# Low-rank rows: transposes spread over later tiles' products, copies in a home of their own, block numbers requested by ScalarE

## The chip, the cores and the metric

The kernel runs on one NeuronCore of a Trainium2 chip. The metric is the device time of one execution in microseconds (us); less is better. Engines are called PE (TensorE), PEld (its weight loads), ACT (ScalarE), DVE (VectorE), POOL (GpSimd) and SP (SyncE, which here only issues DMAs). ACTq and SPq are the DMA-issuing sides of ACT and SP.

## What is computed

`x` has 32 blocks of 32 rows by 512. Four layers are added to it, one after the other; each has a part that is chosen by a number that belongs to the block:

```python
x = x + einsum('bct,bcd->bdt', x, L0_weights[itok_B_0_15])   # L0: one of 16 weights, 32 x 32, per block
base  = einsum('bsi,oi->bso', x, W)                  # L1: one dense 512 x 512 ...
low   = einsum('bsi,bir->bsr', x, lora_A[label])     #     ... and low-rank rows, rank 32, 5 labels
delta = einsum('bsr,or->bso', low, lora_B) * 0.5
x = x + base + delta
x = x + einsum('bsi,boi->bso', x, weight[adapter])   # L2: one of 8 weights, 512 x 512, per block
x = x + attention(x, k_cache, v_cache, block_table, cache_seqlens)   # L3: projections, rotary, attention
```

L3 takes most of the time; the change lies in L0 and L1.

## The kernel before, in words

`stage_layers` does L0, L1 and L2 and prepares L3. The 1024 rows of `x` are TT = 8 tiles of P = 128 rows, four blocks to a tile; KC = 4 chunks of 128 make a row of 512. The stage is one block of code with a stream of its own for each engine; the streams meet at its end (line 271), and the rest of the kernel (`stage_project_attend_output`) begins only then.

The order of the work is a list, `uses` (lines 202 to 210). Each entry is one use of a PSUM bank; entry n has bank `ps[n % 8]`, and PE waits before it until entry n - 8 has been drained (line 359). PE ends each entry with one count on `written`. PE, ACT and DVE all walk the same list in the same order, each doing its own share of an entry. The kinds of entries are:

- ("L0", t): x times the L0 weights of tile t (line 365); DVE adds the bank to x (line 579). The weights of a tile are four 32 x 32 blocks that DVE (tiles 0 to 3, line 549) and ACT (tiles 4 to 7, line 424) copy out of `w0_all` by block number. Both wait first for both DMAs of `idx`, the block numbers (`idx_in`, 32), and read them into registers, then for `w0_all` itself.
- ("x1T", t): four transposes of x (line 369); ACT and DVE split the result into a high and a low part (lines 446 and 587).
- ("low", t): twelve products with `lora_A` of all labels (`a_hi`, `a_lo`); DVE keeps those of the block's own label (line 601) and adds them up into `low` (line 604).
- ("lowT", t): one transpose of `low` (line 382); DVE copies it into `low_t` (line 608).
- ("L1", t): twelve products with W and then one with `bw_t`, the padded `lora_B`, by `low_t` (line 392); DVE adds the bank to x (line 579).
- ("x2T", t): four transposes; ACT copies them into `x2t` (line 472).
- ("L2", t): 64 products, 4 blocks by 4 chunks by 4 (line 402). The weights of blocks 0 to 2 of a tile are copied by DVE and ACT out of `w2t` (`pick`, lines 434 and 537). Those of block 3 come by a DMA of 1 MB that SP issues (`fetch`, line 291), in three buffers; the first is `w1n`.

`low_t` and `bw_t` lie in the room of `a_n`, `a_hi` and `a_lo` (`after_a`), which the low products read. POOL clears `bw_t` (line 330) after the last of them, then fills it (line 333, `bw_ready`).

Before the entry ("L1", 0) DVE runs a block of work that doesn't belong to the list's tiles (lines 557 to 563): `angles`, two `reduce`, and then the first three picks. `angles` also waits for four small DMAs that ACT issues. Its results go to ACT (two sines, line 461), whose results go to POOL (eight tables, line 341, `tables_made`); `w1n` holds the intermediate values. SP waits for `tables_made` 8 before it issues `fetch(0)`, since `fetch(0)` overwrites `w1n`; `fetch(1)` and `fetch(2)` come behind it in SP's order, after the last L1 product.

PE waits before the first product of ("L2", 0) for `x2_turned`, `fetch(0)` and the first picks (lines 394 to 399).

## Time and profile before

| | us |
|---|---|
| median of three runs | 1190.09 |
| lowest and highest | 1187.87, 1191.71 |
| profiled execution, its own time | 1188.03 |
| its span in the profile | 1186.2 |
| busy in the span: PE | 1166.4 |
| DVE | 851.5 |
| POOL | 727.6 |
| ACT | 687.1 |

The profile is of one execution. Its span runs from the first to the last instruction; 1.8 us lie around it. The layers' stage takes the first 105 us of it. Times in the rows are microseconds from the start of the span; "idle before" is how long the engine had done nothing, and the releaser is whatever the profile saw last before it went on. It names one releaser where an instruction waited for several.

### The profile page before, as it was taken

Reading aid. Unit: us, or ns where it says so; the run is one execution under the profiler, and the core shown is the slowest. Engines: PE = TensorE matmul, PEld = TensorE weight load, DVE = VectorE, ACT = ScalarE, POOL = GpSimd, SP = SyncE. Lnnn points to the kernel's source line nnn. Section 1 sums busy time; section 2 is a strip of 40 time slices with the busy share of each in tenths; the row PEclk is TensorE's granted clock in tenths of the full one; section 3 lists DMA queues with packets and bytes.
Section 4 is the critical chain, followed back from the end, with each engine's and each line's share of the span. In section 5 each row is a group of like instructions: output and inputs, shape, how many; then the busy total and the mean of one; then the engine's idle time right before and its main releaser. Section 6 shows DMA issues by size and latency. Waiting matters only on the chain.

```text
span 1186.2 us, 27883 instructions
## 1 busy us (share of the span) xinstructions
PE 1166.4 (98%) x8138; PEld 1030.1 (87%) x8138; DVE 851.5 (72%) x1746; ACT 687.1 (58%) x1647; POOL 727.6 (61%) x566
## 2 busy tenths in 40 slices
PE   7999999999999899999999999999999999999998
PEld 5746888888888799999999999999999998787877
DVE  7878687777866977877878778887788878722222
ACT  4175444344444577777777777777777778412111
POOL 1403999999999765555555555555555556344442
PEclk9999999999999999999999999999999999999999
DMA  9385544534446689999999999999999999876773
GB/s 340 137 279 196 147 134 134 143 82 133 133 125 190 169 256 304 293 298 302 297 301 298 292 304 295 302 296 294 304 295 301 291 334 323 267 218 208 223 212 115
DMA packets 254401, 283.67 MB, mean 239 GB/s; under 512 B 56053, under 2 KB 208629, under 8 KB 254358
## 3 DMA queue, kind: packets, MB, share of 16 engines
q1 hardware_dynamic: 237270, 234.38, 67.6%
q10 hardware_dynamic: 17088, 48.76, 13.5%
q8 instruction: 21, 0.34, 0.1%
q14 instruction: 22, 0.18, 0.1%
HBM read 236.78 MB, written 46.27 MB: 239 GB/s over the span
## 4 chain that ended last, share of the span: by engine, by line
PE 52%; POOL 21%; issue 7%; DMA 5%; DVE 3%; ACT 2%; SPq 0%; ACTq 0%; POOLq 0%; DVEq 0%
PE early_pair L1237 19%; PE early_pair L1212 10%; PE early_pair L109 7%; PE early_pair L110 6%; PE early_pair L111 6%; POOL prj_rstd L1146 6%; POOL prj_qn L1148 5%; POOL prj_ta L1136 5%; DMA all_room_a<-inv_scratch 5%; PE early_pair L1244 3%; POOL prj_rs L1140 3%; POOL all_room_a L1176 2%; DVE out_o_lo L1537 2%; ACT out_o_hi L1728 1%; DVE out_wo_lo L1521 1%
## 5 line engine op out<-in xcount | busy, mean ns | idle before, releaser
L1604 ACT ACTIVATE att_prob<-att_neg,att_nmax 128x544 f32<-128x544 f32 x256 | 192.1, 750 | 115.9 <-DVE att_nmax L1369 91.0
L1369 DVE CUSTOM_DVE_ANT_1 att_neg<-att_mask,early_pair 128x576 f32<-128x576 f32 x256 | 192.1, 751 | 83.3 <-PE early_pair L111 67.5
L1156 POOL TENSOR_TENSOR att_k_lo<-all_room_a,att_k_hi 128x544 fp32r<-128x544 f32 x123 | 165.8, 1349 | 135.4 <-ACT att_k_hi L1630 135.4
L1156 POOL TENSOR_TENSOR att_k_lo<-att_kT,att_k_hi 128x544 fp32r<-128x544 f32 x128 | 173.9, 1359 | 105.5 <-ACT att_k_hi L1630 105.5
L1421 DVE COPY att_pT<-early_pair 128x512 f32<-128x512 f32 x256 | 175.8, 687 | 28.3 <-PE early_pair L1212 28.3
L109 PE MATMUL early_pair<-att_k_hi,att_q_lo 128*128 128x288 f32 (+1 forms) x512 | 168.8, 330 | 1.5 <-DVE att_nmax L1369 1.5
L1212 PE MATMUL early_pair<-all_ident,att_prob 128*128 128x128 f32 x1024 | 157.0, 276 | 0.0
L110 PE MATMUL early_pair<-att_k_lo,att_q_hi 128*128 128x288 f32 (+1 forms) x512 | 147.4, 288 | 0.0
L111 PE MATMUL early_pair<-att_k_hi,att_q_hi 128*128 128x288 f32 (+1 forms) x512 | 147.2, 288 | 0.0
L1176 POOL TENSOR_TENSOR all_room_a<-all_room_a 128x1024 f32<-128x1024 f32 x31 | 78.9, 2545 | 98.7 <-DMA all_room_a<-inv_scratch 98.7
L1237 PE MATMUL early_pair<-att_pT,att_vc 128*128 128x128 f32 x1024 | 135.4, 275 | 0.6 <-ACT att_ost L1761 0.6
L1237 PE MATMUL early_pair<-att_pT,all_room_b 128*128 128x128 f32 x1024 | 135.3, 275 | 0.0
L1212 PEld LDWEIGHTS early_pair<-all_ident,att_prob 128*128 128x128 f32 x1024 | 116.3, 140 | 20.9 <-issue 13.6
L1641 ACT ACTIVATE prj_sq<-early_pair 128x512 f32<-128x512 f32 x64 | 38.3, 599 | 165.5 <-PE early_pair L111 161.4
L1237 PEld LDWEIGHTS early_pair<-att_pT,att_vc 128*128 128x128 f32 x1024 | 124.5, 192 | 0.9 <-ACT att_ost L1761 0.8
L1237 PEld LDWEIGHTS early_pair<-att_pT,all_room_b 128*128 128x128 f32 x1024 | 124.5, 192 | 0.0
L1537 DVE TENSOR_TENSOR out_o_lo<-all_room_a,out_o_hi 128x1024 fp32r<-128x1024 f32 x31 | 41.1, 1325 | 107.7 <-ACT out_o_hi L1728 107.7
L1136 POOL TENSOR_TENSOR prj_ta<-prj_ta,prj_tb 128x640 f32<-128x640 f32 x64 | 101.1, 1579 | 9.1 <-DVE prj_tb L1471 9.0
L109 PE MATMUL early_pair<-out_wo_hi,out_o_lo 128*128 128x512 f32 x256 | 101.1, 395 | 2.5 <-DVE out_o_lo L1537 2.4
L1728 ACT ACTIVATE out_o_hi<-all_room_a 128x1024 fp32r<-128x1024 f32 x31 | 32.8, 1060 | 120.9 <-POOL all_room_a L1176 120.9
L111 PE MATMUL early_pair<-out_wo_hi,out_o_hi 128*128 128x512 f32 x256 | 99.8, 390 | 0.0
L110 PE MATMUL early_pair<-out_wo_lo,out_o_hi 128*128 128x512 f32 x256 | 99.8, 390 | 0.0
(164 smaller groups left out, 2928.7 us busy)
## 6 DMA issues: line engine op xcount, KB each, us to landing
all_room_a<-in_k_cache_t SPq DMA_DIRECT2D x256, 128.0 KB, 5.9
att_kT<-in_k_cache_t SPq DMA_DIRECT2D x256, 128.0 KB, 6.8
all_room_b<-in_L_cond_v_cache SPq DMA_DIRECT2D x136, 128.0 KB, 4.2
q_scratch<-prj_qst SPq DMA_DIRECT2D x64, 256.0 KB
att_vc<-in_L_cond_v_cache SPq DMA_DIRECT2D x128, 128.0 KB, 4.0
att_vc<-in_L_cond_v_cache ACTq DMA_DIRECT2D x128, 128.0 KB, 5.1
all_room_a<-o_scratch SPq DMA_DIRECT2D x31, 512.0 KB, 3.8
all_room_a<-inv_scratch SPq DMA_DIRECT2D x31, 512.0 KB, 5.5
```

What stands on the lines that cost most here:

```text
L109: pe.matmul(out, w_lo, x_hi, start=first, stop=False)
L110: pe.matmul(out, w_hi, x_lo, start=False, stop=False)
L111: return pe.matmul(out, w_hi, x_hi, start=False, stop=last)
L1136: g.tensor_tensor(ta[s][:], ta[s][:], tb[s][:], ALU.add).then_inc(pool_step, 1)
L1146: g.tensor_tensor(rstd[s][:], rs[s][:], power[:], ALU.pow).then_inc(pool_step, 1)
L1156: g.tensor_tensor(k_lo[j % SPLITS][:], kT[j // HK % 2][:, :, j % HK, :], f32(k_hi[j % SPLITS][:]), ALU.subtract).then_inc(k_split, 1)
L1176: g.tensor_tensor(o_n[s], o_n[s], inv_rows[s], ALU.mult).then_inc(o_scaled, 1)
L1212: t = pe.transpose(bank[:, c * P:(c + 1) * P], p[:, c * P:(c + 1) * P], ident[:])
L1237: pe.matmul(o, vc[s][:, c, cols], pT[j % 2][:, c, :], start=(c == 0 and j % PAIR == 0), stop=False)
L1369: v.tensor_tensor_reduce(halves[0], halves[1], scores_of(j, n)[:, :, 0:KA], 1.0, 3.0e38, ALU.add, ALU.min, nmax[j % 2][:]).then_inc(maxed, 1)
L1421: v.tensor_copy(pT[j % 2][:], pt[bank_of(j)][:].rearrange("p (c q) -> p c q", c=NCH)).then_inc(kept, 1)
L1604: act.activation(prob[j // GROUP % 2][:, j % GROUP, :], neg[j % 2][:, 0:KEYS], ACT.Exp, bias=nmax[j % 2][:, 0:1], scale=-1.0, accum_out=to ...
```

## The change

- **Order.** `uses` puts ("lowT", t - 3) behind ("low", t) for t from 3 on, and ("lowT", 5) to ("lowT", 7) behind ("L1", 0). Before, all eight transposes stood between the last low product and the first L1 product. The number of entries is the same.
- **Home.** `low_t` moves out of the room of the `lora_A` parts into the parts of `w2a` that belong to block 3, which the picks don't use.
- **Waits.** PE waits for `low_t` and `bw_t` only ahead of the last product of an L1 entry, no longer ahead of its first.
- **Side work.** DVE's `angles`, `reduce` and first picks, and ACT's sines and first picks, move from ahead of ("L1", 0) to ahead of ("L1", 1).
- **Block numbers.** The two DMAs of `idx` leave SP's queue, where they stood ahead of those of `x`. ACT issues them, one ahead of and one behind that of `w0_all`.

```diff
--- before.py
+++ after.py
@@ -128,7 +128,6 @@
         a_hi = m.sb("a_hi", [P, KC, LR], F32R)
         a_lo = m.sb("a_lo", [P, KC, LR], F32R)
         after_a = Region(nc, "lay", at_a, nc.sbuf_base - at_a)
-        low_t = after_a.sb("low_t", [P, TT, P])
         bw_t = after_a.sb("bw_t", [P, H])
         bw_n = m.sb("bw_n", [R, H])
         lab_i = m.sb("lab_i", [P, B], I32)
@@ -147,6 +146,8 @@
         spare = spare_a[:, 0:2 * H], spare_b[:, 0:2 * H]
         picked = [[w2a[:, r, b] for b in range(BT)] for r in range(2)]
         picked.append([x[:, i * H:(i + 1) * H] for x in spare for i in range(2)])
+        FETCHED = BT - 1
+        low_t = [w2a[:, i // KC, FETCHED, i % KC * P:(i % KC + 1) * P] for i in range(TT)]
         w0_all = w2a[:, 0, 0].rearrange("p (s d) -> p s d", s=NS0)
         x2t = [low[:, i * KC:(i + 1) * KC, :] for i in range(2)]
 
@@ -202,9 +203,10 @@
         uses = [("L0", 0)]
         for t in range(TT):
             uses += ([("L0", t + 1)] if t + 1 < TT else []) + [("x1T", t)]
-        uses += [("low", t) for t in range(TT)]
-        uses += [("lowT", t) for t in range(TT)]
-        uses += [("L1", t) for t in range(TT)] + [("x2T", 0)]
+        for t in range(TT):
+            uses += [("low", t)] + ([("lowT", t - 3)] if t >= 3 else [])
+        uses += [("L1", 0)] + [("lowT", t) for t in range(TT - 3, TT)]
+        uses += [("L1", t) for t in range(1, TT)] + [("x2T", 0)]
         for t in range(TT):
             uses += ([("x2T", t + 1)] if t + 1 < TT else []) + [("L2", t)] + ([("x3T", t - 1)] if t else [])
         uses += [("x3T", TT - 1)]
@@ -221,7 +223,6 @@
                 return split_lo, split_no[u]
             return {"low": low_ready, "lowT": lowt_ready, "x2T": x2_turned}[kind], i + 1
 
-        FETCHED = BT - 1
         BY_ACT, BY_DVE = ((1,), (1, 2), (1,), (1,)), ((0, 2), (0,), (0, 2), (0, 2))
 
         def share_of(share, g):
@@ -272,8 +273,6 @@
 
             @block.sync
             def _(sp):
-                sp.dma_start(idx[:, 0, :], inp["itok_B_0_15"].rearrange("(a b) -> a b", a=1)).then_inc(idx_in, 16)
-                sp.dma_start(idx[:, 1, :], inp["itok_B_3_7"].rearrange("(a b) -> a b", a=1)).then_inc(idx_in, 16)
                 x_rows = inp["x"].rearrange("(t b) c h -> (b c) t h", b=BT)
                 for i in range(X_PARTS):
                     part = slice(i * TT // X_PARTS, (i + 1) * TT // X_PARTS)
@@ -383,13 +382,13 @@
                     elif kind == "L1":
                         pe.wait_ge(split_lo, split_no[("x1T", i)])
                         pe.wait_ge(w1_lo_done, KC)
-                        pe.wait_ge(lowt_ready, i + 1)
-                        pe.wait_ge(bw_ready, 1)
                         tok = slice(i * P, (i + 1) * P)
                         for k in range(KC):
                             three_pass(pe, bank[:], xT_hi[:, k, tok], xT_lo[:, k, tok], w1_hi[:, k, :], w1_lo[:, k, :],
                                        k == 0, False)
-                        end(u, pe.matmul(bank[:], low_t[:, i, :], bw_t[:], start=False, stop=True))
+                        pe.wait_ge(lowt_ready, i + 1)
+                        pe.wait_ge(bw_ready, 1)
+                        end(u, pe.matmul(bank[:], low_t[i], bw_t[:], start=False, stop=True))
                     elif kind == "L2":
                         pe.wait_ge(x2_turned, i + 1)
                         pe.wait_ge(w2_fetched[i % RING], (i // RING + 1) * 16)
@@ -415,7 +414,9 @@
 
             @block.scalar
             def _(act):
+                act.dma_start(idx[:, 0, :], inp["itok_B_0_15"].rearrange("(a b) -> a b", a=1)).then_inc(idx_in, 16)
                 act.dma_start(w0_all, inp["w0_t"]).then_inc(w0_all_in, 16)
+                act.dma_start(idx[:, 1, :], inp["itok_B_3_7"].rearrange("(a b) -> a b", a=1)).then_inc(idx_in, 16)
                 act.wait_ge(idx_in, 32)
                 state = states(mybir.EngineType.Activation, W0_TILES["act"])
                 act.wait_ge(w0_zero, 1)
@@ -455,7 +456,7 @@
                         act.dma_start(len_i[:], inp["itok_B_207_1644"].partition_broadcast(P)).then_inc(rope_in, 16)
                         act.dma_start(nw[:, 0, :], inp["L3_cond_q_norm_w"].partition_broadcast(P)).then_inc(rope_in, 16)
                         act.dma_start(nw[:, 1, :], inp["L3_cond_k_norm_w"].partition_broadcast(P)).then_inc(rope_in, 16)
-                    elif kind == "L1" and j == 0:
+                    elif kind == "L1" and j == 1:
                         act.wait_ge(reduced, 2)
                         for angles in trig:
                             act.activation(angles, angles, ACT.Sin).then_inc(trig_done, 1)
@@ -553,7 +554,7 @@
                     bank, kind, j = ps[i % 8], *u
                     if u == ("x1T", TT - 2):
                         labels()
-                    if u == ("L1", 0):
+                    if u == ("L1", 1):
                         angles()
                         reduce(0, 0.0, 0.0)
                         reduce(1, 0.25, 0.5 * np.pi)
@@ -605,7 +606,7 @@
                                         ALU.add).then_inc(low_ready, 1)
                     elif kind == "lowT":
                         dve.wait_ge(written, i + 1)
-                        v.tensor_copy(low_t[:, j, :], bank[:, 0:P]).then_inc(lowt_ready, 1)
+                        v.tensor_copy(low_t[j], bank[:, 0:P]).then_inc(lowt_ready, 1)
 
 
 def pages_of(nc, table, b, first, count, engine):
```

## Rows read from the trace of the kernel before

**Rows 1.** the page: busy time and share of TensorE, and the chain that ended last by engine

```profile
PE 1166.4 (98%) x8138; PEld 1030.1 (87%) x8138; DVE 851.5 (72%) x1746; ACT 687.1 (58%) x1647; POOL 727.6 (61%) x566
...
PE 52%; POOL 21%; issue 7%; DMA 5%; DVE 3%; ACT 2%; SPq 0%; ACTq 0%; POOLq 0%; DVEq 0%
```

**Rows 2.** waits of SP's queue, 0 to 110 us: waiter, releaser, us in total, times, longest

```profile
SPq L271 <- PEq L271: 3.0, 1, 3.0
```

**Rows 3.** busy time by stretch: PE, PEld, DVE, ACT, POOL, PEclk, DMA share, GB/s

```profile
30.00:40.00 10.00, 8.67 (x43) 6.64 (x42) 8.12 (x34) 0.00 (x0) 2.01 (x2) 1.00 1.01 372
```

**Rows 4.** timeline, 30 to 37 us: start us, us, engine, line, what [idle before <-releaser]

```profile
30.57 0.75 PEld L382 LDWEIGHTS early_pair<-all_ident,lay_low 128*128 128x128 f32 x7
...
33.16 0.19 PEld L109 LDWEIGHTS early_pair<-lay_w,early_xT_lo 128*128 128x128 f32 x1 [1.24 <-DVE lay_low_t L608]
...
35.79 0.41 PEld L392 LDWEIGHTS early_pair<-lay_bw_t,lay_low_t 128*128 128x128 f32 x2
...
36.45 0.19 PEld L109 LDWEIGHTS early_pair<-lay_w,early_xT_lo 128*128 128x128 f32 x1 [0.24 <-issue]
...
36.02 1.02 PE L392 MATMUL early_pair<-lay_bw_t,lay_low_t 128*128 128x512 f32 x2
...
30.85 0.52 POOL L330 MEMSET lay_bw_t<- 128x512 f32 x1 [16.99 <-PE early_pair L111]
31.56 1.49 POOL L333 TENSOR_SCALAR lay_bw_t<-lay_bw_n 32x512 f32<-32x512 f32 x1 [0.19 <-POOL lay_bw_t L330]
...
31.58 1.66 DVE L608 COPY lay_low_t<-early_pair 128x128 f32<-128x128 f32 x8
33.16 0.14 DVE L507 TENSOR_SCALAR lay_row_i<-lay_pos_i 128x1 int32<-128x1 int32 x1
34.44 0.75 DVE L512 CAST lay_pos<-all_len_i 32x8 f32<-32x8 int32 x4 [0.95 <-DMA lay_w1n<-in_L_cond_k_norm_w]
```

**Rows 5.** timeline, 46 to 64 us, from the tables to the first L2 product

```profile
46.16 10.94 POOL L341 TENSOR_TENSOR early_tabs<-lay_w1n 128x512 f32<-128x512 f32 x8 [13.12 <-ACT lay_w1n L461]
...
57.28 0.40 SPq L291 DMA_DIRECT2D lay_w1n<-in_w_t  x1
...
58.84 0.69 DVE L579 TENSOR_TENSOR all_room_a<-all_room_a,early_pair 128x512 f32<-128x512 f32 x1 [1.80 <-PE early_pair L392]
...
62.90 1.09 ACT L472 ACTIVATE lay_low<-early_pair 128x512 f32<-128x512 f32 x2 [13.32 <-PE early_pair L369]
...
63.56 0.15 PEld L402 LDWEIGHTS early_pair<-lay_w2a,lay_low 128*32 128x32 f32 x4 [0.51 <-DVE all_room_a L579]
```

**Rows 6.** loads of block 3's weights: issues of 57 to 62 us; the next two, min/median/max

```profile
lay_w1n<-in_w_t SPq DMA_DIRECT2D x1, 1024.0 KB, 5.5
...
DMA to landing us min/median/max: 5.3/6.7/8.1
```

**Rows 7.** timeline, 0 to 10 us, and the reads of the block numbers

```profile
0.72 0.39 ACTq L418 DMA_DIRECT2D lay_w2a<-in_w_t  x1
...
1.14 0.24 SPq L276 DMA_DIRECT2D lay_idx<-in_itok_B  x1
1.43 1.95 SPq L280 DMA_DIRECT2D all_room_a<-in_x  x4
...
L261 DVEq TENSOR_LOAD <-lay_idx x1: 1358/1358/1358, 3.4 to 3.4; - x1
...
4.99 3.01 DVE L549 COPY early_tabs<-lay_w2a 32x32 f32 x16 [4.99 <-issue]
...
6.27 3.75 PE L365 MATMUL early_pair<-all_room_a,early_tabs 128*128 128x512 f32 x4 [6.27 <-DMA all_room_a<-in_x]
```

**Rows 8.** DMA issues: 0 to 1.5 us (two), and 26 to 27.9 us (one); KB each, landing us

```profile
all_room_a<-in_x SPq DMA_DIRECT2D x1, 512.0 KB, 4.7
lay_w2a<-in_w_t ACTq DMA_DIRECT2D x1, 256.0 KB, 2.7
...
all_len_i<-in_itok_B ACTq DMA_DIRECT2D x1, 16.0 KB, 5.9
```

## The prediction

> **What bounds the kernel now.** I read the busy shares and the chain first. PE is busy for 98% of the span, and the chain that ended last lies half on PE and a fifth on POOL [rows 1]. No part of it names the low-rank rows, so the change can only move the layers' stage as a whole. I then read how that stage ends: SP came to the meeting point and waited 3.0 us for PE's side [rows 2], and nothing of the rest of the kernel starts before. So what counts is by how much PE's last instruction of the stage moves; whatever follows moves with it, one for one.
>
> Then I looked in the stage for time in which PE stood still. The stretch from 30 to 40 us has the hole: 8.67 us busy of 10 [rows 3]. In its timeline PE's weight loads for the eight low-rank transposes begin at 30.57, the first L1 product's load comes at 33.16, and PEld had been idle 1.24 us before it. The profile names DVE's copy as releaser, but L1 (0) needs only the first copy, of about 31.8, while POOL's fill of `bw_t` ended at 31.56 + 1.49 = 33.05. So POOL's `bw_ready` was the late one [rows 4].
>
> The third place is where L1 ends and L2 begins. SP issued `fetch(0)` at 57.28, right behind the last of POOL's eight tables (46.16 + 10.94 = 57.10). ACT copied x2T (0) from 62.90 on, and the first L2 load came at 63.56 [rows 5]. The 1 MB of `fetch(0)` landed 5.5 us after its issue [rows 6], at 62.78. So it was in time by only 0.78 us. That number decides the forecast.
>
> **The transposes and the waits on PE.** Seven transposes' loads took 0.75 us, 0.107 each [rows 4]. Five of them now stand before L1 (0), so its first load comes at 30.57 + 5 x 0.107 = 31.11 instead of 33.16: 2.05 us earlier. Three more stand behind L1 (0), 0.32 us, so from L1 (1) on PE is 1.73 us earlier. All of these are moved, none removed or added. The banks are no new wait: the list is as long as before, and the entries eight places earlier are low products or transposes that DVE has drained by then. What a switch from a transpose to a product costs isn't in the trace at this place; behind the last L1 product PEld paused 0.24 us [rows 4]. So each of five switches costs 0 to 0.24 us, 0 to 1.2 in all; I take 0, because the 1.73 us is not what decides, and keep the 1.2 for the range.
>
> The wait for `bw_ready` moves to L1 (0)'s last product. POOL begins to clear after the last low product, now 4 x 0.107 = 0.43 us later, so `bw_t` is ready at 33.05 + 0.43 = 33.48. It is wanted 35.79 - 33.16 = 2.63 us after L1 (0)'s first load, at 33.74. It is hidden by L1 (0)'s twelve products, with 0.26 us to spare; nothing else waits for it. The new home of `low_t` costs nothing: the same copies by DVE, into a place that nobody uses then. Its purpose is that the copies can come while low products still read the `lora_A` parts. DVE's copies, 1.66 / 8 = 0.21 us each [rows 4], lie in its pauses between low products.
>
> **The side work on DVE.** This is the part that costs. `angles` began at 33.16 (line 507), but had to wait 0.95 us for its small DMAs; without that wait line 512 would have come at 34.44 - 0.95 = 33.49, 0.33 after the start [rows 4]. Now it stands behind L1 (0)'s addition. PE's L1 (0) ended at 36.02 + 1.02 = 37.04, 3.88 after its first load [rows 4], so it ends at 31.11 + 3.88 = 34.99 in the changed kernel. DVE then adds (0.69 [rows 5]) and copies lowT (5) to (7) (3 x 0.21 = 0.63), and begins `angles` at 36.31; line 512 comes at 36.64 instead of 34.44. That is 2.2 us later. Queued behind it on DVE are both reductions and the first picks, and L1's other additions; ACT's sines and picks wait for it, POOL's tables for the sines, and SP's `fetch(0)` for the tables. From line 512 to the issue of `fetch(0)` the work is one chain, 57.28 - 34.44 = 22.84 us, of the same operations as before. So `fetch(0)` is issued at 57.28 + 2.2 = 59.5 and lands 5.5 us later, at 65.0.
>
> The other things that hang on DVE have room. L1's additions after the picks come 2.2 us later, but x2T (0) needs only L1 (0)'s, which is now early, and the first three picks were done before 58.84, when DVE already waited for PE with the L1 additions [rows 5]. SP's own queue is also looked at: `fetch(1)` and `fetch(2)` are issued when L1 ends, about 61 us (ACT copied x2T (0) at 62.90, less 1.73), while `fetch(0)` is in flight. The next two before were issued together and landed after 5.3 and 8.1 us [rows 6], so a load with another right behind it was not slowed: I take 5.5 us, and 8.1 as the other end.
>
> **The meeting of the two.** PE would be ready for L2 (0) at 63.56 - 1.73 = 61.83, and its weights come at 65.0. It waits 3.2 us there, and L2 (0) starts 65.0 - 63.56 = 1.4 us later than before. From there on the same work follows. The hole at 32 us has moved to 62 us and grown.
>
> **The block numbers.** SP no longer issues them, so the first DMA of `x` goes out at 0.72 instead of 1.43. ACT issues numbers, weights, numbers: with the steps of 0.42 us that SP took between such issues (0.72 and 1.14), `w0_all` goes out at 1.14 and the second numbers at 1.56, 0.42 later than before. Before, the numbers and `w0_all` (0.72 + 2.7 = 3.42) were both there at 3.4, when DVE read them; the first block copy came at 4.99, and the four of tile 0 were done at 4.99 + 3.01 / 4 = 5.74. PE started at 6.27, on `x` (1.43 + 4.7 = 6.13) [rows 7, 8]. After, `x` can be there at 5.4, and the copies decide: with the numbers d later, PE starts at 5.74 + 0.1 + d, a shift of h = d - 0.43. How late the second numbers land behind `w0_all`, with `x` in flight beside them, no row shows. The lower end is the issue alone, d = 0.42 and h = 0. The upper end is the nearest small load behind a full stream, 16 KB by ACT that took 5.9 us [rows 8]: 1.56 + 5.9 = 7.46, d = 4.1 and h = 3.6. I take d = 1.0 and h = 0.6, nearer to the lower end, because only the first 512 KB of `x` lie beside it and `w0_all` took 2.7 us with the same `x` arriving. h moves everything after it, `angles` and `fetch(0)` too, since the small DMAs of `angles` have room now.
>
> The Trainium skill ("DMA: Bandwidth & Descriptors", section "Queues, rings and completion order") says that each DMA engine takes turns between the queues it has work for, a whole packet of some 9 to 17 descriptors at a time. At the 372 GB/s of [rows 3] over 16 engines a 2 KB descriptor takes 0.09 us, so a packet of `x` would hold up `w0_all` by an estimated 0.8 to 1.5 us, and the second numbers by as much again. By that rule h would be up to 3.0 us where I take 0.6; no row here shows it, and it is the page behind the second rival.
>
> **The sum.** -1.73 (PE's hole) + 3.2 (the new wait) + 0.6 (the start) = +2.0 us. Against the profiled execution that is 1188.03 + 2.0 = 1190.0; that execution was 2.06 below the median of the runs shown, to which the forecast is made: 1190.09 + 2.0 = 1192.1.
>
> **Rivals.** (1) `fetch(0)` is hidden anyway. Then PE's 1.73 us are a gain: 1190.09 - 1.73 + 0.6 = 1189.0. For it speaks that the hole on PE is real. Against it: L2 (0) would have to be ready later than the load, and the 0.78 us of slack would have to cover 1.73 + 2.2 = 3.9 us. It needs `angles` to start early, or the tables to go faster when their neighbours change. (2) The slower side: the second numbers queue behind `w0_all` and `x`. From h = 2.2 on, that is numbers landing later than about 6.0 us, the loss passes 3.6 us; at h = 3.6 it is 5.0: 1193.7 to 1195.1. For it speaks the 5.9 us row; against it, that the stream is young at 1.5 us. (3) The change doesn't do what it says, because the late one was POOL's `bw_t` and not the transposes: if POOL takes over 0.26 us longer, PE waits at L1 (0)'s last product instead, and `angles` with it. With 0.5 us more it gives 1192.6.
>
> **Chances.** The forecast 0.67, rival 1 0.13, rival 2 0.13, rival 3 0.07. A measurement of this kernel can tell about 0.3%, 3.6 us, from no change. The range goes from rival 1 with h = 0, 1188.4, to rival 2's far end, 1195.1, which also covers the 1.2 us of switches and a `fetch(0)` of up to 8.1 us. Slower by over 0.3%: rival 2, and a little of the forecast for the scatter of the runs (they lay 3.8 us apart), 0.18. Faster by over 0.3%: none of the cases reaches it; scatter alone, 0.03. Within: 0.79.
>
> **What would show it.** In the changed kernel's timeline: the first L1 load near 31.1 + h with almost no idle time before it; line 507 behind L1 (0)'s addition, near 36.3 + h; `fetch(0)` issued near 59.5 + h; a pause of about 3 us on PE before the first L2 product, near 62 to 65; DVE's first block copy at about 6.0 instead of 4.99, and PE's first product at 6.9. The forecast is wrong if L2 (0)'s first load comes before 63.6, if `fetch(0)` is issued before 58, or if the first product waits past 8.

## The result and the profile after

The changed kernel takes 1195.86 us in the median of 15 runs (1193.16 to 1218.33), the kernel before 1190.09 (1186.72 to 1197.75). The ratio is 1.0049, with a 95% interval of 1.0029 to 1.0069: slower by 0.5%, or 5.8 us. The forecast was 1192.1, with a range up to 1195.1, and the side "within 0.3%" as the likeliest. In most kernels here one or two executions were over 1.5% above the fastest; the medians and spreads include them, the ratios leave them out.

The profiled execution of the changed kernel took 1209.45 us, far above its own median; what that is made of comes further down. PE is busy for 7.3 us longer than before, in a span that is 21.4 us longer [rows 1]:

```profile
PE 1173.7 (97%) x8138; PEld 1032.5 (86%) x8138; DVE 862.8 (71%) x1746; ACT 687.0 (57%) x1647; POOL 725.4 (60%) x566
```

The layers' stage again ends with SP waiting for PE [rows 2]:

```profile
SPq L272 <- PEq L272: 2.9, 1, 2.9
```

The start, from the timeline, the read of the block numbers, and the landing of `w0_all` (to be held against [rows 7, 8]):

```profile
0.73 0.54 ACTq L417 DMA_DIRECT2D lay_idx<-in_itok_B  x1
1.31 0.39 ACTq L418 DMA_DIRECT2D lay_w2a<-in_w_t  x1
1.72 0.36 ACTq L419 DMA_DIRECT2D lay_idx<-in_itok_B  x1
...
0.72 2.00 SPq L279 DMA_DIRECT2D all_room_a<-in_x  x4
...
L262 DVEq TENSOR_LOAD <-lay_idx x1: 1347/1347/1347, 6.1 to 6.1; - x1
...
7.66 4.72 DVE L550 COPY early_tabs<-lay_w2a 32x32 f32 x16 [7.66 <-issue]
12.40 1.28 DVE L580 TENSOR_TENSOR all_room_a<-all_room_a,early_pair 128x512 f32<-128x512 f32 x2
...
8.53 3.75 PE L364 MATMUL early_pair<-all_room_a,early_tabs 128*128 128x512 f32 x4 [8.53 <-DVE early_tabs L550]
...
lay_w2a<-in_w_t ACTq DMA_DIRECT2D x1, 256.0 KB, 5.0
```

The numbers are read at 6.1 us instead of 3.4, `w0_all` lands after 5.0 us instead of 2.7, the first block copy comes at 7.66 instead of 4.99 and PE's first product at 8.53 instead of 6.27. DVE's sixteen copies took 4.72 us instead of 3.01. The prediction had named a first product past 8 us as a sign that it is wrong.

The way to the first L2 product, from the timeline (against [rows 4, 5]):

```profile
36.31 0.48 PE L109 MATMUL early_pair<-lay_w,early_xT_lo 128*128 128x512 f32 x1
...
39.13 1.02 PE L391 MATMUL early_pair<-lay_bw_t,lay_w2a 128*128 128x512 f32 x2
...
37.21 1.49 POOL L332 TENSOR_SCALAR lay_bw_t<-lay_bw_n 32x512 f32<-32x512 f32 x1 [0.19 <-POOL lay_bw_t L329]
...
40.20 0.69 DVE L580 TENSOR_TENSOR all_room_a<-all_room_a,early_pair 128x512 f32<-128x512 f32 x1 [2.66 <-PE early_pair L391]
...
41.40 0.14 DVE L508 TENSOR_SCALAR lay_row_i<-lay_pos_i 128x1 int32<-128x1 int32 x1
...
41.76 0.76 DVE L513 CAST lay_pos<-all_len_i 32x8 f32<-32x8 int32 x4
...
64.58 0.40 SPq L290 DMA_DIRECT2D lay_w1n<-in_w_t  x1
...
66.23 1.08 ACT L473 ACTIVATE lay_low<-early_pair 128x512 f32<-128x512 f32 x2 [9.68 <-PE early_pair L368]
...
70.05 1.07 PE L401 MATMUL early_pair<-lay_w2a,lay_low 128*32 128x512 f32 x3 [3.41 <-issue]
...
77.05 0.63 PE L401 MATMUL early_pair<-lay_w2a,lay_low 128*32 128x512 f32 x3
```

and the landing of `fetch(0)`, from the DMA issues (against [rows 6]):

```profile
lay_w1n<-in_w_t SPq DMA_DIRECT2D x1, 1024.0 KB, 5.3
```

Here everything is as worked out, only later by the late start: the L1 products follow the low-rank ones without a hole; `bw_t` is ready at 38.70, ahead of L1 (0)'s last product at 39.13; DVE adds, copies and then begins the side work; `fetch(0)` is issued 7.3 us later than before and lands at 69.9; PE does nothing for 3.4 us and begins L2 at 70.05. The next tile of L2 follows at 77.05, 7.0 us later, where it was 4.5 us before. The reason stands in the stretches (columns: PE, PEld, DVE, ACT, POOL, granted clock, DMA share, GB/s):

```profile
8.00:10.00 2.00, 1.47 (x2) 0.84 (x3) 1.80 (x12) 1.92 (x7) 0.00 (x0) 1.00 0.79 258
...
68.00:70.00 2.00, 0.00 (x0) 0.00 (x0) 0.00 (x0) 0.00 (x0) 0.00 (x0) 0.75 1.04 405
70.00:72.00 2.00, 1.96 (x12) 0.68 (x16) 0.00 (x0) 0.00 (x0) 0.00 (x0) 0.50 1.05 405
74.00:76.00 2.00, 2.00 (x16) 0.45 (x8) 1.04 (x3) 0.92 (x2) 0.00 (x0) 0.54 0.20 77
76.00:78.00 2.00, 2.00 (x24) 0.77 (x20) 1.36 (x3) 1.80 (x4) 0.00 (x0) 1.00 0.00 0
```

In the pause the granted clock falls to 0.50, which is the lower of the two levels (1.2 GHz), and stays there until 75.8 us (0.54 in the mean of 74 to 76), so that most of the first L2 tile runs at half pace. The first stretch, 8 to 10 us, shows the other place with slow products, where the column reads 1.00.

**Marks.** The table holds the moments by which all runs are compared, from their timelines, in us. "Tile" is the time from the first L2 product to that of the next tile; "end" is the first instruction behind the meeting point (POOL's iota). The last columns are the median time and the ratio to the kernel before on the same chip, whose medians were 1190.09, 1189.36 (next four), 1189.95 (four) and 1189.35 (the rest).

| kernel | first copy | PE's first | first selection | first cast of the side work | fetch(0) issued | first L2 | tile | end | median | ratio, 95% interval |
|---|---|---|---|---|---|---|---|---|---|---|
| before | 4.99 | 6.27 | 22.04 | 34.44 | 57.28 | 63.59 | 4.51 | 105.26 | 1190.09 | 1 |
| after | 7.66 | 8.53 | 27.36 | 41.76 | 64.58 | 70.05 | 7.02 | 114.24 | 1195.86 | 1.0049 (1.0029 to 1.0069) |
| idx_back | 5.12 | 6.00 | 22.50 | 36.91 | 59.73 | 65.37 | 5.87 | 108.42 | 1192.00 | 1.0019 (0.9999 to 1.0040) |
| idx_only | 7.59 | 8.46 | 23.95 | 36.98 | 59.82 | 65.53 | 4.53 | 108.40 | 1192.96 | 1.0030 (1.0013 to 1.0047) |
| own_home | 7.59 | 8.47 | 25.13 | 39.54 | 29.50 | 64.71 | 4.43 | 106.30 | 1190.70 | 1.0008 (0.9993 to 1.0024) |
| own_home_idx_back | 5.00 | 5.87 | 22.13 | 36.53 | 29.64 | 61.70 | 4.50 | 103.45 | 1188.66 | 0.9983 (0.9961 to 1.0006) |
| after_again | 7.71 | 8.58 | 24.27 | 38.67 | 61.49 | 66.89 | 5.87 | 109.94 | 1195.08 | 1.0041 (1.0025 to 1.0058) |
| idx_first | 6.70 | 7.58 | 23.92 | 38.33 | 61.15 | 66.61 | 5.88 | 109.65 | 1195.20 | 1.0040 (1.0017 to 1.0062) |
| pool_late | 7.55 | 8.43 | 24.36 | 38.79 | 61.62 | 66.82 | 5.88 | 109.88 | 1195.44 | 1.0048 (1.0030 to 1.0067) |
| side_first | 5.00 | 5.88 | 22.30 | 35.30 | 58.11 | 63.51 | 4.18 | 104.87 | 1189.72 | 1.0010 (0.9988 to 1.0032) |
| side_only | 4.94 | 5.90 | 22.66 | 38.68 | 61.50 | 66.97 | 5.60 | 109.82 | 1195.51 | 1.0037 (1.0004 to 1.0069) |
| x_late | 5.24 | 7.48 | 24.05 | 38.46 | 61.27 | 66.91 | 5.87 | 109.96 | 1193.91 (1 run) | |
| before_again | 5.03 | 5.90 | 22.65 | 34.97 | 57.78 | 64.22 | 4.52 | 105.91 | 1201.57 (1 run) | |
| one_number_first | 3.64 | 4.76 | 21.02 | 35.43 | 29.84 | 60.60 | 4.50 | 102.26 | 1188.22 | 0.9978 (0.9952 to 1.0005) |

The marks of the kernel before moved by up to 0.65 us between two executions, its time by 13.5 us. The end mark of the changed kernel moved by 4.3 us (114.24 and 109.94). Every other kernel has one profile. So what is under 1 us between kernels is read from the marks with care, and what is under 2 to 3 us isn't read from the medians at all.

### The profile page after: what moved, and what is told of

Read it like the earlier page. It is cut to its first block, busy times and chain, and to the rows that moved or that the text cites. A ratio compares the mean times of both kernels' runs of the same rounds, so it can differ in the third digit from the quotient of the medians.

```text
span 1207.6 us, 27883 instructions
## 1 busy us (share of the span) xinstructions
PE 1173.7 (97%) x8138; PEld 1032.5 (86%) x8138; DVE 862.8 (71%) x1746; ACT 687.0 (57%) x1647; POOL 725.4 (60%) x566
## 4 chain that ended last, share of the span: by engine, by line
PE 53%; POOL 20%; issue 7%; DVE 4%; DMA 3%; ACT 2%; ACTq 1%; POOLq 0%; SPq 0%; DVEq 0%
PE early_pair L1238 18%; PE early_pair L1213 9%; PE early_pair L109 7%; PE early_pair L110 7%; PE early_pair L111 7%; POOL prj_rstd L1147 6%; POOL prj_qn L1149 5%; POOL prj_ta L1137 5%; PE early_pair L1245 3%; DMA all_room_a<-inv_scratch 3%; POOL prj_rs L1141 3%; DVE out_o_lo L1538 2%; POOL all_room_a L1177 1%; DVE out_wo_lo L1522 1%; ACT out_o_hi L1729 1%
## 5 line engine op out<-in xcount | busy, mean ns | idle before, releaser
L1177 POOL TENSOR_TENSOR all_room_a<-all_room_a 128x1024 f32<-128x1024 f32 x31 | 76.3, 2462 | 111.6 <-DMA all_room_a<-inv_scratch 111.6
L1538 DVE TENSOR_TENSOR out_o_lo<-all_room_a,out_o_hi 128x1024 fp32r<-128x1024 f32 x31 | 47.3, 1529 | 111.4 <-ACT out_o_hi L1729 111.3
```

The costliest lines, as they stand in the source:

```text
L1177: g.tensor_tensor(o_n[s], o_n[s], inv_rows[s], ALU.mult).then_inc(o_scaled, 1)
```

## The experiments

The two profiles suggested two causes, theory A. The numbers come late, because they are requested behind `w0_all` and beside `x`. And `fetch(0)` comes late, because the side work that releases it stands behind L1 (0); the pause on PE then also costs clock. The rivals: the late numbers are hidden or the order costs all of it (theory B); and other things slow the start (POOL beside DVE's copies).

**The numbers back on SP.** The changed kernel with:

```diff
 def _(sp):
+    sp.dma_start(idx[:, 0, :], ...)
+    sp.dma_start(idx[:, 1, :], ...)
 def _(act):
-    act.dma_start(idx[:, 0, :], ...)
     act.dma_start(w0_all, inp["w0_t"]).then_inc(w0_all_in, 16)
-    act.dma_start(idx[:, 1, :], ...)
```

> The changed kernel with one part undone: SP issues the two requests for the block numbers again, ahead of those of x. Theory A (the numbers came late, and the start of the kernel paid for it twice: PE's first product moved from 6.27 to 8.53 us, and the layer behind it, still at the slow pace, lost about 3 us more): the first low product is back at about 19.9 us, the layers' stage ends about 5.3 us earlier than in the changed kernel (about 108.7 instead of 114.05 us), 1190.5 us in all. The pause before the first L2 product stays at 3 us, the granted clock falls in it, and the first L2 tile takes about 6.5 us instead of 3.5. Theory B (the order on PE and the side work cost it all): the start gets no faster than 1 us, and the time stays at 1195 us or more.

Read of the numbers, and the first L2 product in the timeline:

```profile
L262 DVEq TENSOR_LOAD <-lay_idx x1: 1357/1357/1357, 3.5 to 3.5; - x1
...
65.37 0.63 PE L403 MATMUL early_pair<-lay_w2a,lay_low 128*32 128x512 f32 x3 [3.60 <-issue]
```

The stretch in which that product lies:

```profile
66.00:68.00 2.00, 2.00 (x14) 0.54 (x8) 0.76 (x2) 0.63 (x1) 0.00 (x0) 0.52 0.99 359
```

The numbers are read at 3.5 again, and the first low-rank selection (line 601) is at 22.50, as in the kernel before. The end is at 108.42, where 108.7 was expected; 3.2 us later than before with nothing left of the late numbers. That the number fits is in part luck: it was reckoned from the changed kernel's first profile, with 5.3 us for the start, and against the second one (below) the numbers bring 1.5 us. The median, 1192.00, is above the 1190.5 expected. Theory A holds for the start, not for its size. Of what remains, the first L2 product is 1.8 us late and its tile takes 1.4 us longer, at a granted clock of 0.52 instead of 1.00. I had expected 3 us for that: in the changed kernel's first profile it was 2.5, here and in every other run with the pause 1.1 to 1.4.

**The numbers alone on ACT.** The kernel before with the opposite edit:

```diff
 def _(sp):
-    sp.dma_start(idx[:, 0, :], ...)
-    sp.dma_start(idx[:, 1, :], ...)
 def _(act):
+    act.dma_start(idx[:, 0, :], ...)
     act.dma_start(w0_all, inp["w0_t"]).then_inc(w0_all_in, 16)
+    act.dma_start(idx[:, 1, :], ...)
```

> The kernel before with one part of the change alone: ACT issues the requests for the block numbers, one ahead of and one behind that of w0_all. Theory A: PE's first product comes at 8.5 us instead of 6.3, the first low product 5.3 us later, and since L1 and fetch(0) move together the stage ends 5.3 us later (110.4 instead of 105.06): 1195.4 us. Theory B: the late numbers are taken up by the wait for x and cost under 1 us: 1190 to 1191 us.

```profile
L261 DVEq TENSOR_LOAD <-lay_idx x1: 1351/1351/1351, 6.0 to 6.0; - x1
...
8.46 3.46 PE L363 MATMUL early_pair<-all_room_a,early_tabs 128*128 128x512 f32 x4 [8.46 <-DVE early_tabs L549]
```

The numbers are read at 6.0 and PE starts at 8.46, as in the changed kernel. The end comes 3.1 us later, less than the 5.3 expected: the first selection is 1.9 us late, not 5.3, and the first L2 product still 1.9. The other 1.1 us are one pause before a later tile of L2:

```profile
94.18 0.63 PE L400 MATMUL early_pair<-lay_w2a,lay_low 128*32 128x512 f32 x3 [1.10 <-ACT lay_low L472]
...
lay_w1n<-in_w_t SPq DMA_DIRECT2D x1, 1024.0 KB, 10.2
```

The profile names ACT as releaser, but ACT's copy began at 93.41 and took 0.59 us. That tile also needs the load of its block 3's weights into `w1n`, issued at 83.79. It took 10.2 us (7.9 in the kernel before), so it landed at 94.0, the last of what PE waited for. Why it was slow in this execution isn't shown. A slowdown of 0.30% shows on its own. Theory B, under 1 us, falls; theory A's 5.3 us was too much as well.

**A home of its own for the side work's values.** The changed kernel with:

```diff
-        turns, *trig = (w1n[:, i].rearrange(...) for i in range(3))
-        nw, nw_neg = (w1n[:, 3, ...].rearrange(...) for i in range(2))
+        turns = room[:, 3 * TT * P:3 * TT * P + H].rearrange(...)
+        trig = [after_a.sb(f"trig{i}", [P, TT, HALF])[:] for i in range(2)]
+        nw = nw_room.rearrange(...)          # the last 1 KB of room_a, behind x
+        nw_neg = after_a.sb("nw_neg", [P, 2, D])[:]
...
-                sp.wait_ge(tables_made, 8)
+                sp.wait_ge(w1_lo_done, KC)
                 fetch(0)
...
+                            act.wait_ge(tables_made, 8)
                             split_hi_of_head(0)
```

> The changed kernel with the intermediate values of the side work out of w1n (sines, weights and their negatives in the room of the lora_A parts and behind x, turns in the room of the L0 weights), so that fetch(0) waits only for the split of w1n and not for the tables. Theory A (fetch(0) released late by the tables is what made PE wait before L2, and the wait made the clock fall): no pause before the first L2 product, the granted clock stays at 1.00 there, that tile takes 3.5 us; the stage ends 3.3 us later than in the kernel before instead of 9.0 (5.3 lost at the start, 2.0 gained): about 108.4 us, 1193.4 us in all. Theory B (the clock falls for another reason, or the picks are late too): a pause of over 1 us stays, or the tile stays at 6 us or more.

```profile
29.50 0.40 SPq L292 DMA_DIRECT2D lay_w1n<-in_w_t  x1
...
64.71 0.63 PE L403 MATMUL early_pair<-lay_w2a,lay_low 128*32 128x512 f32 x3 [0.30 <-issue]
```

```profile
64.00:66.00 2.00, 1.70 (x17) 0.68 (x19) 0.33 (x2) 1.17 (x3) 0.00 (x0) 1.00 0.41 125
```

`fetch(0)` is issued at 29.50, and the L2 product no longer waits for it (the 0.30 us idle ahead of it is that of the kernel before). Its tile takes 4.43 us at a granted clock of 1.00, and the end is at 106.30, although the numbers are as late as in the changed kernel. That is 1.0 us later than before instead of the 3.3 expected, because the late start cost 3.1 us by the first selection in this execution, not 5.3. So the pause and the fall of the clock both hang on `fetch(0)`, and the expectation's theory B falls: the picks are not late.

**Both repairs.** The two edits together.

> Both repairs together in the changed kernel: block numbers by SP again, and the side work's values out of w1n so that fetch(0) comes early. If the two causes are all there is, what is left is the gain of the spread transposes: the stage ends at 105.06 - 1.7 = 103.3 us, 1188.4 us in all, no more than 0.15% faster than the kernel before. If something else in the changed order costs time, the stage ends later than 104 us.

```profile
61.70 0.63 PE L405 MATMUL early_pair<-lay_w2a,lay_low 128*32 128x512 f32 x3 [0.30 <-issue]
```

The end is at 103.45, 1.8 us earlier than before, where 1.7 was expected. That is the gain of the spread transposes, left alone. Next to the two causes nothing is left that is larger than the scatter of the marks. In the time of the whole kernel, 0.9983 with an interval that holds 1, it doesn't stand clear.

**The changed kernel again.**

> The changed kernel unchanged, for a second look at its start and its time. In its first profile PE still worked at half pace until 18 us and the stage ended at 114.2 us, 9.0 later than before, more than the 5.8 us between the medians; in two kernels with the same late numbers half pace ended at about 12 us. If that is a matter of the single execution, this profile has its first low-rank selection at 24 to 25.5 us instead of 27.36, and the stage ends at 110 to 112.5. If it belongs to the kernel, it is 27.4 and 114.2 again. Time 1194.5 to 1196.5 us either way.

```profile
7.71 3.45 DVE L550 COPY early_tabs<-lay_w2a 32x32 f32 x16 [7.71 <-issue]
...
66.89 1.04 PE L401 MATMUL early_pair<-lay_w2a,lay_low 128*32 128x512 f32 x3 [3.35 <-issue]
```

First selection at 24.27, end at 109.94, 1195.08 us. So the 114.24 of the first profile belongs to that execution: there the products ran at half pace until 18 us. The 4.3 us between the two at the end are 3.1 by the first selection and 1.1 more in the L2 tile. Of the 3.1, 0.86 are a wait of PE for DVE's addition behind the slow copies. The kernel itself is 4 to 4.7 us late at the end of the stage, which agrees with the 5.1 and 5.8 us of the medians within their intervals.

**Both numbers ahead of `w0_all`.**

```diff
     act.dma_start(idx[:, 0, :], ...)
+    act.dma_start(idx[:, 1, :], ...)
     act.dma_start(w0_all, inp["w0_t"]).then_inc(w0_all_in, 16)
-    act.dma_start(idx[:, 1, :], ...)
```

> The changed kernel with both requests for the block numbers ahead of that of w0_all, all three still by ACT. If the numbers were late because they stood behind w0_all and x, they are read at about 3.5 us now instead of 6.0, and the block copies wait for w0_all alone (issued at 1.7, landing 4.9 later with x beside it, 6.6): first copy at 6.7 instead of 7.6, PE's first product at 7.6 instead of 8.5, 1 us less in all: 1194.5 us. If any small request of ACT's beside x's is slow, they are read at 5 us or later and nothing is gained.

```profile
L262 DVEq TENSOR_LOAD <-lay_idx x1: 1357/1357/1357, 4.1 to 4.1; - x1
...
6.70 3.02 DVE L550 COPY early_tabs<-lay_w2a 32x32 f32 x16 [6.70 <-DMA lay_w2a<-in_w_t]
```

The numbers are read at 4.1 instead of 6.1, and the copies wait for `w0_all`, at 6.70 as expected. PE's first product comes 1.0 us earlier, but the end only 0.3, under the scatter of the marks, and the time is the same (1195.20). What delayed the numbers was their place behind `w0_all`; what delays the copies then is `w0_all` itself.

**x held back.** A probe: in the changed kernel SP waits for `w0_all` ahead of its first request for `x`.

```diff
 def _(sp):
+    sp.wait_ge(w0_all_in, 16)
     x_rows = ...
```

> The changed kernel with SP's first request for x held back until w0_all has landed; a probe of the queue, not a repair. If the numbers were late because x's traffic lay beside w0_all and the numbers behind it, w0_all lands about 2.8 us after its request again (1.31 + 2.8 = 4.1), and the numbers are read at 4.2 to 4.5 us instead of 6.0. If ACT's requests are slow in themselves, they are read at 5.5 us or later. x then comes at 4.1 + 4.7 = 8.8 us, so the stage isn't faster.

```profile
L262 DVEq TENSOR_LOAD <-lay_idx x1: 1351/1351/1351, 3.6 to 3.6; - x1
...
lay_w2a<-in_w_t ACTq DMA_DIRECT2D x1, 256.0 KB, 2.6
```

With no transfer beside it, `w0_all` lands after 2.6 us (4.7 to 5.0 beside `x`), and the numbers behind it are read at 3.6. So the lateness is the traffic of `x` on the same DMA engines, not the issuing engine. This is one execution, and its time is not used.

**POOL behind the copies.** In the changed kernel POOL's two operations on the `lora_A` parts fell into DVE's copies.

```diff
                 pool.wait_ge(a_in, 16)
+                pool.wait_ge(w0_placed["dve"], TT // 2)
```

> The changed kernel with one wait added on POOL: its two operations on the lora_A parts start only when DVE has placed its blocks. In the changed kernel they fell into DVE's sixteen copies, which took 4.7 us instead of 3.0. If they slow the copies down, the copies take 3.0 to 3.1 us now (7.6 to 10.7), DVE's first addition comes at about 10.8 instead of 12.4, and the first transposes follow without the pause: 1.2 us gained or more, 1194 us. POOL ends by about 13.2 then, still ahead of the first low product at 22 us. If the copies are slow for another reason they stay at 4.7 us.

```profile
7.55 3.02 DVE L551 COPY early_tabs<-lay_w2a 32x32 f32 x16 [7.55 <-issue]
10.60 0.69 DVE L581 TENSOR_TENSOR all_room_a<-all_room_a,early_pair 128x512 f32<-128x512 f32 x1
```

The copies take 3.02 us again, so POOL beside them does cost DVE's copies 1.7 us in the changed kernel's first profile (0.4 in its second). But the selection is at 24.36 and the end at 109.88, as in the changed kernel's second profile. PE's own slow products of the first two tiles set that place there. The expected gain of 1.2 us didn't come in the median either, 1195.44: a miss. Where the copies took 4.7 us, in the changed kernel's first profile and in own_home (4.69), PE did wait 0.84 to 0.86 us for DVE's addition behind them, and own_home's selection was 0.8 us later, at 25.13. So POOL costs up to 0.9 us at the start in some executions, and none in others.

**The side work alone.** The kernel before, with only the side work moved behind L1 (0):

```diff
-                    elif kind == "L1" and j == 0:
+                    elif kind == "L1" and j == 1:
...
-                    if u == ("L1", 0):
+                    if u == ("L1", 1):
```

> The kernel before with one part of the change alone: the side work (angles, reductions, first picks, sines) behind L1 (0) instead of ahead of it. Nothing is gained on PE. By the working as corrected so far: L1 (0) ends at 37.04, DVE adds until 37.7, the first cast comes at 38.1 instead of 34.44, 3.7 us later; fetch(0) is issued at 61.0, lands at 66.3, and the first L2 product comes at 66.4 instead of 63.59, after a pause of 3 us. In the pause the granted clock falls, which costs 1.4 us more in the first L2 tile. The stage ends 4.2 us later than before, at 109.5: 1194 us. If the fall of the clock belongs to something else in the changed kernel, the stage ends at 108.1.

```profile
61.50 0.40 SPq L291 DMA_DIRECT2D lay_w1n<-in_w_t  x1
...
66.97 1.07 PE L402 MATMUL early_pair<-lay_w2a,lay_low 128*32 128x512 f32 x3 [3.04 <-issue]
```

```profile
66.00:68.00 2.00, 1.03 (x8) 0.44 (x12) 0.00 (x0) 0.00 (x0) 0.00 (x0) 0.62 0.90 286
```

End at 109.82 against 109.5 expected, a pause of 3.04 us, and a granted clock of 0.62 in the stretch, in a kernel whose start and transposes are those of before. This one step in the order ends the stage as late as the whole change (109.94), in which the gain of the transposes and the late start nearly cancel. It is the test of the corrected working, and it held by the marks; the median, 1195.51, stands clear of the kernel before, but its ratio's interval is the widest here.

**The side work ahead of L1 (0) again.** The changed kernel with the numbers on SP and this order; PE does the last low-rank transpose behind the twelve products of L1 (0), ahead of its last one:

```diff
-            uses += [("low", t)] + ([("lowT", t - 3)] if t >= 3 else [])
-        uses += [("L1", 0)] + [("lowT", t) for t in range(TT - 3, TT)]
-        uses += [("L1", t) for t in range(1, TT)] + [("x2T", 0)]
+            uses += [("low", t)] + ([("lowT", t - 2)] if t >= 2 else [])
+        uses += [("lowT", t) for t in range(TT - 2, TT)]
+        uses += [("L1", t) for t in range(TT)] + [("x2T", 0)]
...
-                    if u == ("L1", 1):
+                    if u == ("L1", 0):
```

> Block numbers by SP; the side work stands ahead of L1 (0) again, and so all transposes stand ahead of it in DVE's order: (lowT, t - 2) behind (low, t), and PE does the last transpose only behind the twelve products of L1 (0), ahead of its last product. Theory (moving the side work behind L1 (0) is what let fetch(0) come late): the side work's first cast is at 34.4 to 35 us, fetch(0) is issued at 57.3 to 57.8 and lands at about 63, PE is ready for L2 at 61.9 and waits 1 us instead of 3.5; the granted clock stays at 1.00 through the first L2 tile; the stage ends at 104.3 to 105.0, 0.3 to 1 us earlier than before: 1189 us. Rival: if PE's pause of 1 us already lets the clock fall, the stage ends at 107 or later.

```profile
35.30 0.76 DVE L516 CAST lay_pos<-all_len_i 32x8 f32<-32x8 int32 x4
...
58.11 0.40 SPq L292 DMA_DIRECT2D lay_w1n<-in_w_t  x1
...
63.51 0.63 PE L406 MATMUL early_pair<-lay_w2a,lay_low 128*32 128x512 f32 x3 [1.93 <-issue]
```

```profile
62.00:64.00 2.00, 0.49 (x8) 0.24 (x12) 0.00 (x0) 0.27 (x1) 0.00 (x0) 1.00 1.03 312
64.00:66.00 2.00, 2.00 (x24) 0.72 (x20) 1.16 (x4) 1.04 (x2) 0.00 (x0) 1.00 0.99 352
```

The cast is at 35.30, `fetch(0)` at 58.11, both a little later than expected, and PE waits 1.93 us instead of 1. The clock stays at 1.00, and the end is at 104.87, 0.4 us earlier than before, which is under the scatter of the marks. It is the changed kernel's idea without its cost, and the kernel's time is that of before. The spread transposes gain nothing as long as `fetch(0)` waits for the tables, since the 1.7 us won on PE turn into the wait.

**One number first.** Both repairs, and SP requests the L2 numbers only behind `x`:

```diff
     sp.dma_start(idx[:, 0, :], ...).then_inc(idx_in, 16)
-    sp.dma_start(idx[:, 1, :], ...).then_inc(idx_in, 16)
     for i in range(X_PARTS):
         sp.dma_start(x[:, part], x_rows[:, part]).then_inc(x_in[i], 16)
+    sp.dma_start(idx[:, 1, :], ...).then_inc(ids2_in, 16)
...
-    dve.wait_ge(idx_in, 32)
+    dve.wait_ge(idx_in, 16)
```

> An attempt at a version better than both: both repairs (side work's values out of w1n, block numbers by SP), and in addition only the L0 numbers ahead of x, the L2 numbers behind x with a semaphore of their own, waited for only where they are used. The L0 numbers and w0_all were there at 3.4 us and the first copy at 5.0; without the second request the numbers may come 0.4 us earlier, but w0_all (0.72 + 2.7 = 3.4) sets the copies then, after a read of the numbers that is over earlier. First copy at 4.6 to 4.9, PE's first product at 5.5 to 5.8, stage end 103.0 to 103.5, 1188 us; not to be told from the version with both repairs by its time, only by its marks.

```profile
L265 DVEq TENSOR_LOAD <-lay_idx x1: 1353/1353/1353, 2.0 to 2.0; - x1
...
3.64 3.01 DVE L555 COPY early_tabs<-lay_w2a 32x32 f32 x16 [3.64 <-DMA lay_w2a<-in_w_t]
...
4.76 3.75 PE L369 MATMUL early_pair<-all_room_a,early_tabs 128*128 128x512 f32 x4 [4.76 <-DMA all_room_a<-in_x]
```

The numbers are read at 2.0 us, and the copies start at 3.64 as soon as `w0_all` is there. The end is at 102.26, 3.0 us earlier than before and 1.2 earlier than with both repairs, more than expected. By the medians it is the fastest of all, 1188.22; its ratio, 0.9978, has an interval of 0.9952 to 1.0005, so that it beats the kernel before is shown by the marks and not by the time.

**The kernel before again.**

> The kernel before, a second look at its stage marks: how far they move from one execution to the next. First low-rank selection within 0.6 us of 22.04, stage end within 0.6 us of 105.26. If they move by more than 1 us, the differences of under 1 us between the experiments mean nothing.

The marks agree: 22.65 and 105.91. But this execution took 1201.57 us, and its last part has pauses on PE, with the granted clock down:

```profile
1140.00:1160.00 20.00, 16.56 (x65) 12.93 (x65) 8.90 (x5) 4.24 (x4) 7.62 (x4) 0.91 0.50 135
```

The changed kernel's first profile had the same kind at another place:

```profile
1100.00:1105.00 5.00, 2.54 (x12) 1.79 (x11) 3.86 (x2) 2.12 (x2) 2.36 (x1) 1.00 0.05 20
```

These pauses in the output stage come and go in both kernels. Of the 14.5 us by which the changed kernel's first span is longer than its second (1207.6 and 1193.1), 4.3 lie in the layers' stage and the rest behind it, most of it in such pauses. In them PE waited for DVE, DVE for ACT, ACT for POOL, and POOL for a load into `all_room_a`, up to 8.5 us (4.1 at the longest in about the same part of the kernel before). Why those loads are late at times stays open.

## Why the prediction was wrong

**PE's hole: right.** L1 was to begin 2.05 us earlier and PE to be 1.73 us ahead from L1 (1) on. With the start and `fetch(0)` out of the way (own_home_idx_back) the end came 1.8 us earlier (2.5 against the second execution of the kernel before). The switches between transposes and products cost nothing that shows: the first L1 product follows the transpose at once.

**`bw_t`: right.** Hidden by 0.4 us (38.70 against 39.13, from 0.26 worked out); rival 3 had no part.

**The side work: right.** The cast was to come 2.2 us later than before; in idx_back it came 2.5 later, of which 0.5 is the scatter of the start. `fetch(0)` was issued 2.45 us later and PE took it up 5.6 us after its issue, so the next fetches behind it hardly slowed it (5.5 was taken). The first L2 product came 1.8 us late where 1.4 plus the start was said. Rival 1 was disproved by the pause in every run that kept the order, and shown as the right picture of a kernel in which `fetch(0)` is free.

**The pause: half seen.** The prediction put a pause of 3.2 us on PE and priced it as time that passes. It has a second price: the granted clock fell to the lower level in it, or within 0.8 us of its end, and was there for most of the next tile. That is the step "from there on the same work follows". Measured: 5.87 us a tile instead of 4.5, so 1.4 us were missing from the sum. The kernel before has no row that prices it, but it should have been a term bounded from 0 to one tile's length, since the tile twice as slow would be 4.5 us more.

**The block numbers: wrong, and the largest miss.** I took d = 1.0 and h = 0.6, and rival 2, with a chance of 0.13, began at h = 2.2. Measured: the first copy 2.7 us later, PE's first product 2.26, which is rival 2 at its near edge. The failing step is the reason for staying near the lower end, "`w0_all` took 2.7 us with the same `x` arriving". It hadn't: before, SP asked for `x` 0.71 us behind `w0_all`; after, 0.59 us ahead of it (0.72 against 1.31). Beside `x`, `w0_all` took 5.0 us and landed at 6.3; the numbers, requested behind it at 1.72, were read at 6.1. The probe with `x` held back gave 2.6 us and a read at 3.6. So the second numbers took 4.4 us from request to read, about midway between the 2.8 that I had taken and the row of 5.9. That the delay passed to the end in part only (1.9 us by the first selection in idx_only, of 2.3 at PE's first product) fits the slow first products: they lasted 4.0 us from PE's first in the kernel before and 3.0 us in idx_only, so the late start was paid in part by fewer of them.

The estimate from the Trainium skill ("DMA: Bandwidth & Descriptors", section "Queues, rings and completion order") gave h up to 3.0, against my 0.6; the traces have 2.26, inside it. For `w0_all` alone it gave 0.8 to 1.5 us, and the traces have 2.0 to 2.3. So of the estimate the total holds here and the share of `w0_all` doesn't, and no run shows the packets themselves.

**The sum, corrected.** 1.4 (the meeting of PE and `fetch(0)`) + 1.9 (the start, as the first selection of idx_only has it) + 1.4 (the clock) = 4.7 us: 1190.09 + 4.7 = 1194.8. The stage end is 4.0 to 4.7 us late in the changed kernel's second profile; the median, 1195.86, is 1.1 us above the sum, within its interval of 3.5 to 8.2 us. Of the 2.7 us between this sum and the forecast's 2.0, 1.4 are the clock, for which there was no term, and 1.3 the start. The missing term is also why the range ended 0.8 us too low: its upper end took the start's far end (5.0 us in all) but no clock, and with 1.4 us more it would be 1196.5. The chance of slower by over 0.3% was set at 0.18 only.

## What to carry to other kernels

Work that is taken off the path of one engine isn't a gain until the next thing to be late is later than the gain; here a buffer shared by a side computation and a prefetch held the release, and moving the side work by one entry cost more than the hole had. Price a new pause of about 3 us on TensorE twice, by its length and by the slower products behind it. A small request that many wait for belongs ahead of large ones, alone: behind 256 KB and beside the loads of `x` it came 2.7 us later, and without its unneeded sister 1.4 us earlier.

## What the runs showed of the hardware

- After each pause of 3.0 to 3.6 us before the first L2 product the granted clock fell to 0.50: in the changed kernel's first profile 1.0 us ahead of the product, in x_late 0.8 us behind it. It stayed there for more than half of the tile, in that first profile twice as long as in the others. After the pause of 1.93 us in side_first it read 1.00 throughout. In the output stage it also fell behind a pause of 2.8 us (one_number_first, near 1163 us), and didn't behind one of 2.5 us (the changed kernel's first profile, near 1103 us).
- At the start of every run the first four L0 products took 3.5 to 3.75 us (two take 1.02 later). The column of the granted clock reads 1.00 there, but it only counts what is recorded, and the trace's first record of the clock, at full, begins where the slow products end. That was at 12.4 us in one profile of the changed kernel and at 17.8 in the other. PE had stood idle for 0.86 us in the one that ended late, but in own_home it had too (0.84), and was at full pace from 13.1 us. What ends it stays open.
- Two requests in a row for 128 bytes each were both there at 3.4 us; the first alone at 2.0. A request of 256 KB landed after 2.6 to 2.8 us with `x` asked for behind it or held back, and after 4.7 to 5.0 with `x` asked for ahead of it.
- Sixteen small DVE copies took 3.0 us alone and 3.5 to 4.7 with two POOL operations beside them.
